# Part of pair 6's expert work moved into the last pair's tail, and the last value product cut in other parts

## The reference

```python
h = tok(x, ...)
h = h + attn(layernorm(h), Wq, Wk, Wv, Wo)
# features = layernorm(h)
rh = relu(features @ router_w1 + router_b1)
logits = softmax(rh @ router_w2 + router_b2)
top_w, top_i = top_k(logits, 2); routing = softmax(top_w)
h1 = relu(einsum('bsd,edh->bseh', features, expert_w1) + expert_b1)   # 6 experts
h2 = relu(einsum('bseh,ehf->bsef', h1, expert_w2) + expert_b2)
out = einsum('bseh,eho->bseo', h2, expert_w3) + expert_b3
h = h + sum over the two chosen experts of out * routing
```

## Time and profile before

| what | value |
|---|---|
| median of 3 runs | 717.21 us |
| the profiled execution | 715.59 us, span 713.8 us |
| TensorE | busy 656.0 us, 92% of the span, 11790 products |
| VectorE, ScalarE, GpSimd | 77%, 66%, 39% |
| mean granted clock of TensorE | 0.985 |
| chain that ended last | TensorE 62%, VectorE 20%, ScalarE 6%, issue 5%, GpSimd 5% |

### The profile page before, as it was taken

The page is one execution under the profiler, slowest core; times in us unless marked ns, Lnnn a source line. Parts: engine busy times, 40 slices in busy tenths (PEclk is TensorE's granted clock), DMA queues, the critical chain, the costliest instruction groups (busy, mean ns, idle before and its releaser), DMA issues.

```text
span 713.8 us, 27054 instructions
## 1 busy us (share of the span) xinstructions
PE 656.0 (92%) x11790; PEld 376.0 (53%) x11790; DVE 549.3 (77%) x1080; ACT 472.6 (66%) x1186; POOL 280.6 (39%) x354
## 2 busy tenths in 40 slices
PE   6589999999999999999999999999999999999974
PEld 5436555545655465444655466454655456445652
DVE  6678777878787887878787887978778786878535
ACT  2378885877568755886658766687658875776422
POOL 1333115404752176511953146521755028305402
PEclk9799999999999999999999999999999999999988
DMA  4000000000000000000000000000000000000000
GB/s 176 1 3 2 2 2 3 3 1 3 17 3 2 2 3 18 2 2 2 7 15 2 2 3 17 2 2 3 3 17 2 2 2 18 2 2 3 17 3 17
DMA packets 9430, 6.96 MB, mean 10 GB/s; under 512 B 8672, under 2 KB 8800, under 8 KB 9184
## 3 DMA queue, kind: packets, MB, share of 16 engines
q1 hardware_dynamic: 9312, 5.23, 2.6%
HBM read 3.13 MB, written 2.10 MB: 7 GB/s over the span
## 4 chain that ended last, share of the span: by engine, by line
PE 62%; DVE 20%; ACT 6%; issue 5%; POOL 5%; DMA 1%; SPq 0%; ACTq 0%; DVEq 0%; POOLq 0%
PE s_bank L522 24%; PE s_bank L491 18%; DVE nmax L893 7%; PE s_bank L606 4%; ACT p L779 4%; DVE e2t L1104 3%; PE s_bank L681 3%; PE s_bank L670 2%; PE s_bank L503 2%; DVE st L910 2%; ACT e1t L827 2%; DVE hatt L1089 1%; PE s_bank L703 1%; PE s_bank L532 1%; PE s_bank L585 1%
## 5 line engine op out<-in xcount | busy, mean ns | idle before, releaser
L779 ACT ACTIVATE p<-s_bank,nmax 128x512 f32<-128x512 f32 x512 | 347.9, 691 | 153.5 <-DVE nmax L893 152.1
L893 DVE TENSOR_REDUCE nmax<-s_bank 128x1 f32<-128x512 f32 x512 | 325.9, 680 | 51.2 <-PE s_bank L491 50.6
L491 PE MATMUL s_bank<-kf,g 64*64 64x512 f32 x2048 | 261.7, 594 | 6.9 <-ACT p L779 3.2
L522 PE MATMUL s_bank<-p,woz 64*64 64x256 f32 x4096 | 246.8, 378 | 9.5 <-POOL woz L344 5.0
L522 PEld LDWEIGHTS s_bank<-p,woz 64*64 64x64 f32 x4096 | 163.3, 133 | 125.3 <-issue 43.9
L344 POOL TENSOR_TENSOR woz<-cst,rz 128x256 f32<-128x256 f32 x126 | 74.5, 612 | 251.9 <-DVE rz L899 251.9
L491 PEld LDWEIGHTS s_bank<-kf,g 64*64 64x64 f32 x2048 | 73.6, 133 | 89.9 <-issue 46.0
L779 ACT ACTIVATION_READ_ACCUMULATOR p<-s_bank,nmax 128x1 f32 x512 | 105.2, 206 | 0.0
L1192 POOL TENSOR_TENSOR st<-st,power 128x8 f32<-128x8 f32 x24 | 42.9, 1787 | 64.6 <-DVE st L920 64.6
L905 DVE STREAM_TRANSPOSE m<-s_bank 128x512 f32<-128x512 f32 x64 | 45.5, 712 | 24.1 <-PE s_bank L522 24.1
L353 POOL TENSOR_TENSOR y<-y,gt 128x768 f32<-128x768 f32 x28 | 41.3, 1475 | 28.5 <-DVE gt L1073 28.1
(11 more groups left out here) (117 smaller groups left out, 527.7 us busy)
## 6 DMA issues: line engine op xcount, KB each, us to landing
tower_out<-o SPq DMA_DIRECT2D x16, 128.0 KB, 2.8
cst<-consts SPq DMA_DIRECT2D x1, 1198.0 KB, 9.0
e2t<-ids SPq DMA_DIRECT2D x1, 896.0 KB, 6.3
cst<-consts SPq DMA_DIRECT2D x1, 544.0 KB, 4.6
cst<-consts SPq DMA_DIRECT2D x1, 288.0 KB, 6.6
e2t<-ids SPq DMA_DIRECT2D x1, 128.0 KB, 2.3
cst<-consts SPq DMA_DIRECT2D x1, 4.5 KB, 2.1
```

The source lines that it names most:

```text
L491: last = pe.matmul(double[half(q), 512 * r:512 * r + 512], g[half(r), a // 2 % 2, a % 2, first:first + 64], kf[half(r), par, a // 4, :], s ...
L522: last = pe.matmul(bank("PV", i, a)[half(q), 512 * hh:512 * hh + 256], woz[half(r), kept, 2 * mm + hh, :], keys[:, q, :, :], start=(part = ...
L779: nc.scalar.activation(p[:, 8 * kept + c % 8, :], bank("S", i, c - r)[:, 512 * r:512 * r + 512], ACT.Exp, bias=nmax[:, c % 16:c % 16 + 1], ...
L893: nc.vector.tensor_reduce(nmax[:, c % 16:c % 16 + 1], bank("S", i, c - r)[:, 512 * r:512 * r + 512], AX.X, ALU.max, negate=True).then_inc( ...
```

## The change

- Table `Z`: pair 6's E1 are in slots 44, 47 and 54 (before 28, 32, 39), its E2 in 59, 62 and 63, with VectorE's copies in 58, 64 and 66, its Y in 65, 72, 75 and 77, with VectorE's part in 69, 71, 74 and 77. Slots of 64 and more lie in the tail, where all four engines now call pair 6's ffn ahead of pair 7's.
- The value product of the tail: part 0 has batch half 0 with all eight heads and half 1 with four; parts 1 and 2 are half 1 alone, two heads each. Part 1 moves from slot 11 to 0, part 2 from 19 to 9.
- `WARM_T`: 12 for 20.
- Of the tail's E2, ScalarE copies the first half and VectorE the second, all three in slot 35; a new semaphore `e2_first` counts ScalarE's.
- Table `L` has other slots throughout. The order of pair 7's own steps on TensorE stays the same.

```diff
-WARM0, WARM, WARM_T = 18, 13, 20
+WARM0, WARM, WARM_T = 18, 13, 12
 Z = {'FIN': 11,
- 'LN': 10,
+ 'LN': 11,
  'SQ': 15,
- 'LN2': 17,
- 'T': 23,
- 'T_ACT': 23,
- 'R': 25,
- 'R_ACT': 25,
- 'L': 26,
- 'GATE': (28, 28, 29, 32, 38, 44, 44),
- 'GATE_ACT': (28, 38),
- 'E1': (28, 32, 39),
- 'E1_ACT': (31, 34, 39),
- 'E2': (33, 39, 40),
- 'E2_DVE': (33, 39, 40),
- 'Y': (43, 47, 51, 56),
- 'Y_DVE': (42, 47, 53, 58)}
+ 'LN2': 16,
+ 'T': 22,
+ 'T_ACT': 20,
+ 'R': 23,
+ 'R_ACT': 23,
+ 'L': 24,
+ 'GATE': (26, 26, 29, 31, 36, 42, 43),
+ 'GATE_ACT': (25, 36),
+ 'E1': (44, 47, 54),
+ 'E1_ACT': (45, 47, 54),
+ 'E2': (59, 62, 63),
+ 'E2_DVE': (58, 64, 66),
+ 'Y': (65, 72, 75, 77),
+ 'Y_DVE': (69, 71, 74, 77)}
 L = {'FIN0': 63,
- 'FIN1': 11,
- 'FIN2': 19,
- 'LN': 9,
- 'SQ': 4,
- 'LN2': 16,
- 'T': 22,
- 'T_ACT': 7,
- 'R': 25,
- 'R_ACT': 13,
- 'L': 40,
- 'GATE': (22, 34, 34, 39, 41, 45, 51),
- 'GATE_ACT': (28, 45),
- 'E1': (26, 43, 44),
- 'E1_ACT': (14, 30, 42),
- 'E2': (44, 48, 56),
- 'E2_ACT': (38, 43, 46),
- 'Y': (57, 62, 63, 63),
- 'Y_DVE': (56, 57, 61, 62)}
+ 'FIN1': 0,
+ 'FIN2': 9,
+ 'LN': 7,
+ 'SQ': 0,
+ 'LN2': 8,
+ 'T': 12,
+ 'T_ACT': 9,
+ 'R': 13,
+ 'R_ACT': 9,
+ 'L': 28,
+ 'GATE': (14, 24, 31, 31, 31, 37, 61),
+ 'GATE_ACT': (18, 32),
+ 'E1': (23, 42, 45),
+ 'E1_ACT': (15, 19, 24),
+ 'E2': (43, 50, 55),
+ 'E2_ACT': (28, 39, 53),
+ 'E2_DVE': (35, 35, 35),
+ 'Y': (57, 60, 62, 63),
+ 'Y_DVE': (61, 62, 63, 63)}
@@ value products
-            def value_products(i, par, first, end):
+            def value_products(i, par, *heads):
                 for n in range(8):
                     for g4 in range(4):
                         q, s2 = g4 // 2, g4 % 2
-                        for b2 in range(2):
+                        for b2, first, end in heads:
...
-                value_products(i, par, *((0, 4), (4, 6), (6, 8))[n]).then_inc(fin_parts, 1)
+                value_products(i, par, *(((0, 0, 8), (1, 0, 4)), ((1, 4, 6),), ((1, 6, 8),))[n]).then_inc(fin_parts, 1)
@@ the tail of TensorE (ScalarE, VectorE and GpSimd get the same call)
                 products(PAIRS, slot, False, True)
+                ffn(PAIRS - 2, 0, slot + SLOTS, Z)
+                ffn_out(PAIRS - 2, slot + SLOTS, Z)
                 ffn(PAIRS - 1, 1, slot, L)
@@ ScalarE's copies of the tail's E2
-                        for r in range(2):
-                            last = nc.scalar.activation(e2t[:, 2 * e + r, :], bank("E2", i, e)[:, 512 * r:512 * r + 512],
-                                                        ACT.Relu, bias=k("e2b")[:, 2 * e + r:2 * e + r + 1])
-                        last.then_inc(e2_sb, 1)
+                        nc.scalar.activation(e2t[:, 2 * e, :], bank("E2", i, e)[:, 0:512], ACT.Relu,
+                                             bias=k("e2b")[:, 2 * e:2 * e + 1]).then_inc(e2_first, 1)
@@ VectorE's
-                    if f is not L and slot == f["E2_DVE"][e]:
+                    if slot == f["E2_DVE"][e]:
                         dve.wait_ge(e2_ps, EP * i + e + 1)
-                        for r in range(2):
+                        for r in ((1,) if f is L else (0, 1)):
```

More of the change, by code:

```diff
@@ L91 @@
 Z = {'FIN': 11,
- 'LN': 10,
+ 'LN': 11,
  'SQ': 15,
- 'LN2': 17,
- 'T': 23,
- 'T_ACT': 23,
- 'R': 25,
- 'R_ACT': 25,
- 'L': 26,
- 'GATE': (28, 28, 29, 32, 38, 44, 44),
- 'GATE_ACT': (28, 38),
- 'E1': (28, 32, 39),
- 'E1_ACT': (31, 34, 39),
- 'E2': (33, 39, 40),
- 'E2_DVE': (33, 39, 40),
- 'Y': (43, 47, 51, 56),
- 'Y_DVE': (42, 47, 53, 58)}
-L = {'FIN0': 63,
- 'FIN1': 11,
- 'FIN2': 19,
- 'LN': 9,
- 'SQ': 4,
  'LN2': 16,
  'T': 22,
- 'T_ACT': 7,
- 'R': 25,
- 'R_ACT': 13,
- 'L': 40,
- 'GATE': (22, 34, 34, 39, 41, 45, 51),
- 'GATE_ACT': (28, 45),
- 'E1': (26, 43, 44),
- 'E1_ACT': (14, 30, 42),
- 'E2': (44, 48, 56),
- 'E2_ACT': (38, 43, 46),
- 'Y': (57, 62, 63, 63),
- 'Y_DVE': (56, 57, 61, 62)}
+ 'T_ACT': 20,
[10 more added lines that the diff above has]
+ 'Y_DVE': (69, 71, 74, 77)}
+L = {'FIN0': 63,
+ 'FIN1': 0,
[17 more added lines that the diff above has]
+ 'Y_DVE': (61, 62, 63, 63)}
 def at(slot, offset, i):
@@ L195, in ring_order @@
             order.append(("PV", *found))
+        ffn(PAIRS - 2, slot + SLOTS, Z)
         ffn(PAIRS - 1, slot, L)
@@ L218, in read_at @@
     if name in ("E1", "E2", "Y"):
-        reader = "E1_ACT" if name == "E1" else "Y_DVE" if name == "Y" else "E2_ACT" if f is L else "E2_DVE"
+        reader = "E1_ACT" if name == "E1" else "Y_DVE" if name == "Y" else "E2_DVE"
         slot = f[reader][e]
@@ L317, in tower @@
             sem(x) for x in ("tok_half", "fin_ps", "fin_parts", "hatt_sb", "x2t_ps", "xt_sb", "rh_ps", "rh_sb", "l_ps", "gate", "gate_act")]
-        (e1_ps, e1_sb, e2_ps, e2_sb, y_ps, y_sb, y_pool, y_dve, gated) = [
-            sem(x) for x in ("e1_ps", "e1_sb", "e2_ps", "e2_sb", "y_ps", "y_sb", "y_pool", "y_dve", "gated")]
+        (e1_ps, e1_sb, e2_ps, e2_sb, e2_first, y_ps, y_sb, y_pool, y_dve, gated) = [
+            sem(x) for x in ("e1_ps", "e1_sb", "e2_ps", "e2_sb", "e2_first", "y_ps", "y_sb", "y_pool", "y_dve", "gated")]
         LN_DVE, LN_STEP = 4, (4, 3, 3)
@@ L476, in free @@
                     pe.wait_ge(e2_sb, EP * i + e + 1)
+                    if i + 1 == PAIRS:
+                        pe.wait_ge(e2_first, e + 1)
                 if name == "Y":
@@ L626, in ffn @@
                     free("FIN", i, 1)
-                    value_products(i, par, 0, HEADS).then_inc(fin_ps, 1)
+                    value_products(i, par, (0, 0, HEADS), (1, 0, HEADS)).then_inc(fin_ps, 1)
                 for n in (1, 2):
@@ L698, in ffn_out @@
                             pe.wait_ge(e2_sb, EP * i + EP)
+                            if f is L:
+                                pe.wait_ge(e2_first, EP)
                         for x in range(NE):
```

## The result

The changed kernel takes 712.57 us (median of 8 runs, 710.92 to 714.3) against 717.79 for the kernel before (8 runs beside it): ratio 0.9938, 95% interval 0.9921 to 0.9955. Beside the experiments it was measured once more: 0.9933 (0.9915 to 0.9952). By the ratios it is faster by 4.5 and 4.8 us, with intervals of some 3 to 6; the two medians are 5.2 apart. The forecast was 5.6.

What follows compares the result with a forecast made beforehand. The prediction took TensorE to bound the body, with a serial end behind the last scores. Its terms, 0.65 - 3.9 - 2.0 - 0.35 = -5.6 us, gave 711.6 us against the median of 717.21, range 708.8 to 715.8.

Steps and rivals of the forecast that it cites:

- sum A: Body to the end of the last context product: +0.65 us, bounds -1.0 and +2.0.
- sum D: From the transposes to the last store: -0.35 us, bounds -0.5 and +0.5.
- fetch limit: TensorE's instruction fetch needs 2.8 to 3.5 us per 128 pairs; a 1.0 us hole at the last context product's head.
- Sum B: From the last context product's end to the residual additions: 1.95 us instead of 5.84, -3.9.
- Sum C: From the residual additions to the transposes: -2.0 us, down to -1.5, with 24 warming instructions instead of 40.
- The shared copies give almost nothing: Gating behind the transposes: halving ScalarE's copies lengthens VectorE's chain; first output at 11.2 us, before 11.29.
- 1: Rival: clock falls in the transposes, through router, logits and first expert; 2.6 us more, 714.2 us; chance 0.24.
- 2: Rival: fetch holes stay behind the context product; gain only 3.2 us, 714.0 us; chance 0.10.
- 3: Rival: clock stays at 1.2 GHz from the transposes to the last output; 4.1 us slower, 721.3 us; chance 0.04.
- 4: Rival: the body has another bound than TensorE, adding 3 us there; 714.6 us; chance 0.10.

Runs made afterwards that it cites:

- c1: The changed kernel again without an edit, timed and profiled as control beside the experiments: ratio 0.9933 to the kernel before.
- e4: The changed kernel with `WARM_T` back at 20 from 12: ratio 0.9941 to the kernel before.
- e5: The changed kernel with GpSimd's weighted sums of pair 6's outputs 2 and 3 replaced by 2-element additions, those rows not computed: ratio 0.9891.
- e6: The changed kernel with ScalarE copying both halves of the last pair's second layers again, `e2_first` waits gone: ratio 0.9923.
- e10: The changed kernel with the bias of pair 6's outputs 2 and 3 added on TensorE and VectorE multiplying them by the gate: 710.05 us, ratio 0.9900.
- e11: e10 with ScalarE copying both halves of the last second layers: 711.5 us, ratio 0.9925.
- e3: The changed kernel with table `Z` of before, so all of pair 6's expert work is back in the last body: ratio 0.9955.
- e2: The kernel before with only `WARM_T` changed, 12 for 20: ratio 0.9977.
- e1: The kernel before with only the value product's parts changed, slots as before: ratio 0.9955.
- e7: The changed kernel with only outputs 2 and 3 of pair 6 in the tail, ahead of the transposes, and the rest back in the body: ratio 0.9942.
- e8: e7 with ScalarE copying both halves of the last second layers: ratio 0.9952.
- e9: e7 with `WARM_T` 20 and GpSimd's last weighted sum waiting until the normalised tile is made: 710.21 us, ratio 0.9912.

## Why the prediction was right or wrong

The time and the sign held; the gain was forecast at 5.6 and is 4.5 to 5. In part that is luck: two errors stand against each other, sum A too high by 1.65 us and sum D too low by 3.5 in the first profile (2.1 in c1).

- **The fetch limit: right in place, varying in size.** The hole expected at the head of the last context product stands behind its first record, 0.53 us idle and 0.91 from start to start where 0.06 is usual, so 0.85 lost where 1.0 was summed. It stands behind that first record in all kernels with the same count of pairs ahead of it (changed, c1, e4, e5, e6, e10: 0.42 to 0.62 us idle; e11: only 0.07, and its body is 0.35 shorter), and elsewhere where the count is another. Counted from the program's first product record, every one of these holes stands ahead of a record whose number is a multiple of 128: 11008 in those seven, 11136 in e3, 11264 and 11392 in the kernel before and in e2. That the limit is the fetch is argued from this and from the packets; no run tests it. The least time for 128 pairs is no fixed 2.8 to 3.5 us: e1 passed record 11264 without a hole 2.65 us behind record 11136, and e2 needed 3.75 with one. (The block that the prediction puts at "about 2.8" took 2.94, from 674.94 on.) How many blocks the engine holds at a time, no run shows.
- **Sum A: sign wrong.** +0.65 summed, -1.0 measured. Parts 0 and 1 together took 4.55 for 2.02 (+2.5, 2.25 summed), output 0 and the hole were as summed. But part 0 began 5.2 us earlier, where 3.3 were summed: TensorE was busy for 59.98 of the body's 61.42 us, against 63.71 of 66.61. The holes in the body fell from 2.9 to 1.4 us, and the busy time by 3.7 where I had priced the four output products at 2.8, start to start. That had gone into the bounds, not into the sum. Where the further 0.9 us of busy time went isn't traced.
- **Sum B: right.** 2.06 where 1.95 was summed; e1 shows that it is the parts' doing, and not the move's.
- **Sum C: right in size (-1.7 for -2.0), wrong in cause.** I gave it to the fewer warming products. e4 shows that they are worth nothing there; e1 shows that the clock at 2.4 GHz, behind a shorter idle time, wins it all without them. Where the clock is down, fewer of them do help (e2). 0.3 us were lost because GpSimd held the centring L937 too (0.99 for 0.69); GpSimd's own L367 beside it took 0.90 for 0.45.
- **Sum D: the step that failed.** -0.35 summed, +3.2 measured, and +1.75 in c1. I followed GpSimd's sums for what waits on them (the power, the store), and never for what runs beside them. The sums stretched the gating by 2.4 us (gone in e5), and so the first gated output left 13.32 us behind the transposes, not 11.2. The half clock of the first outputs cost another 1.4: that is how much longer this end is than c1's, whose first gated output left at the same 13.33. The clock fell there behind gaps of 2.84 and 2.87 us (changed, e4) and in no kernel with 2.02 or less; that the gap is the cause isn't tested by itself. "The shared copies give almost nothing" holds for neither case: in the changed kernel they cost 0.6 to 0.8 us, and with the gating clean they gain, 10.82 us to the first gated output in e3 against 11.29 before, and 1.0 and 1.8 us of "end" in e10 and e7 against e11 and e8.
- **Rivals.** 1, the fall of the clock in the transposes, came in c1, e5, e7 and e8, not in the first profile; the price was 1.2 to 1.9 us at the logits, not 2.6, and in the changed kernel it hides behind GpSimd. It is a matter of the execution: the clock fell behind gaps of 2.32 and 2.33 us (c1, e5) and stayed up behind one of 2.32 in the first profile and in e6. 2, 3 and 4 did not come.

## What to carry to other kernels

Work moved off the busy engine into a tail has to be followed on every engine it takes along: here, of the 4 us that TensorE saved in the body, 2.4 came back as GpSimd's sums beside VectorE's small operations. A chain of many small two-operand VectorE operations is the worst place for long GpSimd ones; give those less work (2.4 us for 4 in e10), or start them behind the operation they would hold (e9). And before warming products are cut or added, look at whether the clock is already up when they start.

## What the runs showed of the hardware that I had not expected

- A VectorE operation of 0.21 us with two SBUF operands, begun 0.02 us behind a GpSimd one of 1.47, took 1.52: it is held to about the other's end, not slowed in proportion. One of 0.69, begun 0.07 us behind the same kind, took 1.95 and ended 0.55 behind it (e7). GpSimd's operations are held too: 0.45 became 0.90 beside L937. VectorE's operations with one operand in PSUM (L1097, 1.42 us beside GpSimd and 1.41 before) and its reductions (L1043, 0.20) kept their times.
- The same code's first 600 us differed by up to 2.5 us between executions (603.34 to 605.83 at pair 6's value product), while the next 61.4 us, to the last pair's value product, repeated within 0.02 in the changed kernel, c1, e4, e5, e6, e10 and e11. Stages of two profiles are to be compared from a common point behind such a difference.
- Value products of two heads of one batch half took 1.16 us for 64 records alone (changed kernel), against 1.61 for 128 of both halves and 2.09 for 128 of one half (e1): half the records are not half the time, and records of the two halves go faster together than as many of one.
